# The end of a state-space layer's y (skip term D·xc and gate silu(z)) on ACT and POOL instead of PE and DVE

## The reference, cut to what matters

```
xs, z = split(u @ W_in.T)                  # 192 + 192 channels
xc = silu(causal_conv3(xs) + conv_b)
dt, B, C = split(xc @ W_x.T)               # 6 + 16 + 16
delta = softplus(dt @ W_dt.T + b_dt)
h_t = exp(delta*A) * h_(t-1) + delta*B*xc  # 192 channels x 16 states
y = sum_n h*C  +  xc * D
y = y * silu(z)
out = x + y @ W_out.T
```

## Time and profile before

| | us |
|---|---|
| median of 3 runs (7182.05 to 7199.08) | 7185.96 |
| the profiled execution | 7219.16 |
| its span, first to last instruction | 7217.5 |
| PE busy | 6447.3 |
| DVE busy | 5943.6 |
| ACT busy | 4794.1 |
| POOL busy | 4577.4 |

### The profile page before, as it was taken

The page is one execution under the profiler, slowest core; times in us unless marked ns, Lnnn a source line. Parts: engine busy times, 40 slices in busy tenths (PEclk is TensorE's granted clock), DMA queues, the critical chain, the costliest instruction groups (busy, mean ns, idle before and its releaser), DMA issues. The chain is left out here.

```text
span 7217.5 us, 97516 instructions
## 1 busy us (share of the span) xinstructions
PE 6447.3 (89%) x32099; PEld 3299.1 (46%) x32099; DVE 5943.6 (82%) x4956; ACT 4794.1 (66%) x7986; POOL 4577.4 (63%) x4516
## 2 busy tenths in 40 slices
PE   7898998999898998999999899998999989898765
PEld 5545444444444444444444444444444444444211
DVE  0188888888888888888888888888888888889898
ACT  4576767667676776766667666676766767667554
POOL 0166666666666766667666666666766666677676
PEclk8998989999898998999999898998989999899776
DMA  3465655655655555565655555666555655555552
GB/s 89 112 151 134 146 141 129 148 136 146 148 136 141 140 143 137 145 147 131 150 130 147 143 134 140 138 150 144 136 146 132 150 137 145 144 129 142 121 122 68
DMA packets 805815, 983.15 MB, mean 136 GB/s; under 512 B 391258, under 2 KB 417542, under 8 KB 805318
## 3 DMA queue, kind: packets, MB, share of 16 engines
q1 hardware_dynamic: 805318, 976.92, 56.4%
HBM read 717.71 MB, written 259.00 MB: 135 GB/s over the span
## 5 line engine op out<-in xcount | busy, mean ns | idle before, releaser
L1069 POOL TENSOR_TENSOR hc<-hs,cs 128x512 f32<-128x512 f32 x3072 | 3843.5, 1269 | 2272.8 <-DVE hs L1028 1880.1
L1028 DVE TENSOR_TENSOR_SCAN hs<-av,state,b 128x512 f32<-128x512 f32 x2688 | 3282.4, 1264 | 83.5 <-DVE b L1022 2.7
L1022 DVE TENSOR_TENSOR b<-rep_u,pb 128x1536 f32<-128x1536 f32 x1024 | 1802.8, 1761 | 785.3 <-PE pb L746 721.2
L883 ACT ACTIVATE av<-rep_d,nega 128x512 f32<-128x512 f32 x3072 | 2129.2, 713 | 139.4 <-DVE hs L1028 134.9
L757 PE MATMUL py<-hc,rsel 128*32 128x512 f32 x6144 | 1227.4, 678 | 27.3 <-POOL hc L1069 27.2
L676 PEld LDWEIGHTS cb<-w2c,g 128*98 128x98 f32 x9600 | 937.6, 178 | 330.2 <-issue 267.9
L671 PE MATMUL cb<-xu,w1a 96*128 96x392 f32 x2400 | 1039.9, 529 | 50.1 <-ACT dlt L873 31.0
L676 PE MATMUL cb<-w2c,g 128*98 128x96 f32 x9600 | 990.2, 264 | 83.2 <-issue 55.4
L833 ACT ACTIVATE g<-cb,b1a 128x392 f32<-128x392 f32 x1200 | 695.7, 580 | 205.3 <-PE cb L671 189.5
L746 PE MATMUL pb<-bc,selb 96*128 96x512 bf16 x1024 | 416.4, 407 | 370.0 <-DVE b L1022 368.6
L710 PE MATMUL cb<-xn,wtap 96*96 96x512 f32 x1536 | 701.0, 606 | 0.3 <-DVE spare L966 0.3
(11 more groups left out here) (102 smaller groups left out, 6525.5 us busy)
## 6 DMA issues: line engine op xcount, KB each, us to landing
rep_d<-delta_scratch SPq DMA_DIRECT2D x512, 384.0 KB, 6.2
rep_u<-deltax_scratch SPq DMA_DIRECT2D x512, 384.0 KB, 6.1
cs<-c_scratch SPq DMA_DIRECT2D x512, 256.0 KB, 6.1
delta_scratch<-dlt SPq DMA_DIRECT2D x128, 384.0 KB, 3.1
deltax_scratch<-dlt SPq DMA_DIRECT2D x128, 384.0 KB, 8.1
t_scratch<-t1s SPq DMA_DIRECT2D x128, 300.0 KB
t1r<-t_scratch SPq DMA_DIRECT2D x160, 240.0 KB, 5.0
rr<-v_scratch SPq DMA_DIRECT2D x256, 150.0 KB
```

Of the source, the lines that this page charges most:

```text
L883: act.activation(av[:, n % NAV, :], rep_d[:, k % 2, j, :], ACT.Exp, scale=nega[:, q, j:j + 1])\
L1022: dve.tensor_tensor(b3[:, :, :], rep_u[:, k % 2, 3 * hf:3 * hf + 3, :], pb[:, None, :].broadcast_to([128, 3, T]), ALU.mult).then_inc(dve_b ...
L1028: dve.tensor_tensor_scan(hs[:, n % NHS, :], av[:, n % NAV, :], b3[:, n % 3, :], start, ALU.mult, ALU.add)\
L1069: pool.tensor_tensor(hc[:, n % NHC, :], hs[:, n % NHS, :], cs[:, k % 2, g % NQ, :], ALU.mult)\
```

## The change

`ddiag` and its matmul go; `gate` goes from DVE. In their place:

- ACT scales xc by D in place (Copy with a scale per partition, SBUF to SBUF, both halves) behind its unit 16, one chunk ahead.
- ACT copies `py` (half 0 behind its unit 21, half 1 behind unit 9 of the next chunk) to a new SBUF tile `yv`. PE waits for that copy (`act_y`) before it starts the next half in `py`, where it waited for the gate.
- POOL adds `yv` to the scaled xc and multiplies by `zs`, two instructions in place, behind its unit 17 (half 0) and unit 5 of the next chunk (half 1). OUT and Z's evacuation wait for that (`pool_g`).
- OUT moves in the plan from position 6 to 11, so that ACT evacuates it behind unit 17, and SP stores it and loads `x1o` at its unit 19 instead of 13.

```diff
-    "act": dict(xn=8, mid=23, batch=BATCH + 6),
-    "dve": dict(y0=15, y1=3),
-    "pool": dict(u=23, bc=(16, 21)),
-    "sp": dict(..., x1=21, out=13),
+    "act": dict(xn=8, y=(21, 9), d=16, mid=23, batch=BATCH + 6),
+    "dve": dict(),
+    "pool": dict(u=23, bc=(16, 21), y=(17, 5)),
+    "sp": dict(..., x1=21, out=19),
...
-        rows.append((k * NU + 6, ("PAD", -1) if kind == "first" and k == 0 else ("OUT", k)))
+        rows.append((k * NU + 11, ("PAD", -1) if kind == "first" and k == 0 else ("OUT", k)))
...
                 if q == 0:
-                    pe.wait_ge(dve_y, count(dve_y, G * 2 + hf))
-                    pe.matmul(py[0:C, :], ddiag[:, hf, :], xcs[:, k % 4, hf, :], start=True, stop=False,
-                              skip_group_check=True)
+                    pe.wait_ge(act_y, count(act_y, G * 2 + hf))
                 for j in range(3):
                     mm = pe.matmul(py[32 * j:32 * j + 32, :], rsel[:, :], hc[:, (3 * g + j) % NHC, :],
-                                   start=False, stop=(q == NQ - 1), skip_group_check=True)
+                                   start=(q == 0), stop=(q == NQ - 1), skip_group_check=True)
...
+            def c_part(st, k, n):
+                if n == AT["act"]["d"] and 0 <= st.s * NC8 + k + 1 < NS * NC8:
+
+                    for hf in range(2):
+                        xc = xcs[:, (k + 1) % 4, hf, :]
+                        act.wait_ge(pool_u, count(pool_u, st.s * NC8 + k + 2))
+                        act.activation(xc, xc, ACT.Copy, scale=dskip[:, hf:hf + 1]).then_inc(act_d, 1)
+
+                G = st.s * NC8 + k - (AT["act"]["y"].index(n) if n in AT["act"]["y"] else 0)
+                if n in AT["act"]["y"] and not (G < 0) and not (n == AT["act"]["y"][0] and k == NC8):
+                    hf = AT["act"]["y"].index(n)
+                    act.wait_ge(pool_y, count(pool_y, G * 2 + hf))
+                    act.wait_ge(pe_red, count(pe_red, G * NG + (hf + 1) * NQ))
+                    act.activation(yv[:, :], py[0:C, :], ACT.Copy).then_inc(act_y, 1)
...
-                if n == AT["dve"]["y0"]:
-                    gate(G, k, 0)
-
-            def gate(G, k, hf):
-
-                dve.wait_ge(pe_red, count(pe_red, G * NG + (hf + 1) * NQ))
-                dve.tensor_tensor(xcs[:, k % 4, hf, :], zs[:, k % 2, hf, :], py[0:C, :], ALU.mult).then_inc(dve_y, 1)
...
+                xc = xcs[:, G % 4, hf, :]
+                pool.wait_ge(act_d, count(act_d, G * 2 + 2))
+                pool.wait_ge(act_y, count(act_y, G * 2 + hf + 1))
+                pool.tensor_tensor(xc, xc, yv[:, :], ALU.add).then_inc(pool_y, 1)
+                pool.wait_ge(pool_y, count(pool_y, G * 2 + hf + 1))
+
+                pool.tensor_tensor(xc, xc, zs[:, G % 2, hf, :], ALU.mult).then_inc(pool_g, 1)
```

More of the change, by code:

```diff
@@ L36 @@
     "pe": dict(pb=1, red=5),
-    "act": dict(xn=8, mid=23, batch=BATCH + 6),
-    "dve": dict(y0=15, y1=3),
-    "pool": dict(u=23, bc=(16, 21)),
-    "sp": dict(rd=(1, 2, 3, 5), ru=(6, 8, 10, 12), cs=(15, 16, 17, 18), dl=20, du=4, x1=21, out=13),
+    "act": dict(xn=8, y=(21, 9), d=16, mid=23, batch=BATCH + 6),
+    "dve": dict(),
+    "pool": dict(u=23, bc=(16, 21), y=(17, 5)),
+    "sp": dict(rd=(1, 2, 3, 5), ru=(6, 8, 10, 12), cs=(15, 16, 17, 18), dl=20, du=4, x1=21, out=19),
 }
@@ L114, in plan_of @@
             rows += mamba_rows(k, True)
-        rows.append((k * NU + 6, ("PAD", -1) if kind == "first" and k == 0 else ("OUT", k)))
+        rows.append((k * NU + 11, ("PAD", -1) if kind == "first" and k == 0 else ("OUT", k)))
     if kind == "last":
-        rows.append((NC8 * NU + 6, ("OUT", NC8)))
+        rows.append((NC8 * NU + 11, ("OUT", NC8)))
     return padded(rows)
@@ L185, in build @@
         dskip = sb("dskip", [C, 2])
-        ddiag = sb("ddiag", [C, 2, C])
         selb = sb("selb", [C, NQ, 128], BF16)
@@ L241, in build @@
         os_ = sb("os_", [128, 4, C])
+        yv = sb("yv", [C, T])
         cb = ps("cb", [128, RING, 512])
@@ L290, in build @@
         pe_red = sem("pe_red")
-        dve_y = sem("dve_y")
+        act_y = sem("act_y")
+        act_d = sem("act_d")
+        pool_y = sem("pool_y")
+        pool_g = sem("pool_g")
         out_st = sem("out_st")
@@ L325, in build @@
         SETUP_STEPS = 3
-        N_SETUP = 14
+        N_SETUP = 12
         BEFORE = [alone([("SLD", 0)] + s_steps() + [("SG1", 0), ("SG2", 0)]),
@@ L730, in out @@
                 p = (k - 1) % 4
-                pe.wait_ge(dve_y, count(dve_y, G * 2))
+                pe.wait_ge(pool_g, count(pool_g, G * 2))
                 pe.wait_ge(x1o_ld, count(x1o_ld, G * 16))
@@ L859, in batched @@
                     t = key[2]
-                    act.wait_ge(dve_y, count(dve_y, (G2 - LEAD) * 2))
+                    act.wait_ge(pool_g, count(pool_g, (G2 - LEAD) * 2))
                     act.wait_ge(pe_conv, st.done(i))
@@ L912, in when @@
                 return row[0] + LAG["act"]
-            run(when, unit, step, a_part, lambda st, k, n: None)
+            def c_part(st, k, n):
[10 more added lines that the diff above has]
+                    act.activation(yv[:, :], py[0:C, :], ACT.Copy).then_inc(act_y, 1)
+            run(when, unit, step, a_part, c_part)
         @block.vector
@@ L940, in _ @@
                                         cwb.rearrange("c (p t k) -> c k t p", t=2, k=3)[:, tap], ALU.mult))
-            for t in range(2):
-                setup(dve.tensor_scalar(ddiag[:, t, :], ident[0:C, 0:C], dskip[:, t:t + 1], None, ALU.mult))
             dve.wait_ge(setup_a, count(setup_a, 2))
@@ L1029, in unit @@
                     .then_inc(dve_h, 1)
-                if n == AT["dve"]["y0"]:
-                    gate(G, k, 0)
-            def gate(G, k, hf):
-                dve.wait_ge(pe_red, count(pe_red, G * NG + (hf + 1) * NQ))
-                dve.tensor_tensor(xcs[:, k % 4, hf, :], zs[:, k % 2, hf, :], py[0:C, :], ALU.mult).then_inc(dve_y, 1)
[L1038 to L1043, removed]
+            run(lambda row: row[0] + LAG["dve"], unit, step, lambda st, k, n: None, lambda st, k, n: None)
         @block.gpsimd
@@ L1102, in a_part, with c_part @@
                     pool.tensor_tensor(dlt[:, :, :], dlt[:, :, :], xcs[:, k2 % 4], ALU.mult).then_inc(pool_u, 1)
-            run(lambda row: row[0] + LAG["pool"], unit, step, a_part, lambda st, k, n: None)
+            def c_part(st, k, n):
+                if n not in AT["pool"]["y"]:
+                    return
+                hf = AT["pool"]["y"].index(n)
+                G = st.s * NC8 + k - hf
+                if G < 0 or (hf == 0 and k == NC8):
+                    return
+                xc = xcs[:, G % 4, hf, :]
[4 more added lines that the diff above has]
+                pool.tensor_tensor(xc, xc, zs[:, G % 2, hf, :], ALU.mult).then_inc(pool_g, 1)
+            run(lambda row: row[0] + LAG["pool"], unit, step, a_part, c_part)
 def resampling():
```

## The result

The changed kernel takes 7226.5 us (median of 18 runs, 7172.3 to 7282.8) and the kernel before, in runs beside them, 7189.5. The ratio is 1.0048, with a 95% interval of 1.0033 to 1.0064: 0.5% slower, where I had forecast 1.6% faster. One of the 18 runs, that of 7282.8 us, lies over 1.5% above the fastest and counts as slow; the ratio is taken over the other 17. The profiled execution has a span of 7244.9 us at a mean granted clock of 0.89; before it was 0.91.

The account below looks back on a forecast made before the run. PE and DVE were taken to hold each other through the one `pb` bank. Per chunk -2.0 + 0.8 + 0.3 = -0.9 us, times 128, plus 2.4 once: 7186 - 113 = 7073 us, range 6955 to 7215.

Parts of the forecast that it names:

- The scaling, 0.8 us a chunk: ACT's two scalings by D delay the evacuation PE needs at OUT: bounds 0 and 1.6 us a chunk, middle taken.
- the worked chunk: Chunk 0, worked step by step between spreads of B: waits 5.55 us against 6.49, chunk 2.1 us shorter with the gates.
- The base, -2.0 us a chunk: Gain on PE and DVE from dropping diagonal matmul and gate and moving OUT: between 1.14 and 2.0 us, 2.0 taken.
- SP's store and load move with OUT and cost nothing: On SP, OUT's store and the load of `x1o` come six units later: priced at nothing.
- POOL and the copies, 0.3 us a chunk: ACT's copies of `py` and POOL's four instructions a chunk: bounds 0 and 1.3 us, taken near the lower end.
- the fifth rival: POOL feeds PE late at `reduce` behind unit 5 or 20, a 2.5 us pair in most chunks: up to 7390; chance 0.08.
- The third: Behind the batch, OUT and ACT's late evacuation cost 1.6 + 0.3 us a chunk nearly everywhere: about 7173; chance 0.20.
- The fourth: PE waits ahead of group 3's spread, so the batch (X, Z) runs partly at half clock: about 7285; chance 0.12.
- the prediction's own paragraph on the clock: After PE waits, its records run at half clock (1.2 GHz); so a batch could start at half clock.

Follow-up runs that it names:

- the kernel with the scalings out of the way: Changed kernel with ACT's two scalings by D behind unit 14 instead of 16: 7059.4 us, ratio 0.9807 to the kernel before.

## Why the prediction was wrong

Two terms of the sum were mis-sized, and both in the hopeful direction. Per chunk I had -2.0 + 0.8 + 0.3.

- **The scaling, 0.8 us a chunk, was 1.36** (174 us over 128 against the place behind unit 14). This is the step that failed: the rows gave a bound of 1.6 us in the worked chunk, the wait came out at 1.45 and 1.71, and I took the middle for want of the other chunks. I also priced only the wait. The waits themselves are some 0.5 us a chunk, which is below the middle; the half clock behind them adds up to 0.9 (both estimates, from the two ways of splitting above). The longer W_2 record of chunk 3 is that part.
- **The base, -2.0 us a chunk, with POOL's 0.3 was to give -218 us; the kernel with the scalings out of the way gives -139.** The worked chunk 0 and chunk 1 of the earlier trace rows stood for all eight. By chunk, that kernel gains 1.7 to 3.6 us in chunks 1, 2, 4, 6 and 7, 0.5 in chunk 3, 0.1 in chunk 0, and loses 2.9 in chunk 5. The diagonal matmul alone brings 92 us and not 256: in chunks 0, 5 and 6 nothing is left of it, and a later stretch of each runs longer at a lower clock. In the worked chunk 0, where I forecast 2.1 us, the last stretch is 1.8 us longer with the scalings at 14 (10.1 against 8.3 on average), its granted clock 0.67 against 0.90; what lowers the clock there is open. And about 3 us of each chunk 5, some 45 us in all, go to the wait for `rr`, which I had not seen: I wrote that SP's store and load move with OUT and cost nothing, and did not ask what OUT and the diagonal matmul had covered on PE.
- Either error alone would have stayed in the range: 7073 + 72 = 7145 and 7073 + 79 = 7152. Together they are 7224. That this meets the measured 7226.5 confirms nothing, since both are measured against the same kernel, the one with the scalings at 14, and must add up to the difference. What the scalings cost behind unit 14 themselves, if anything, counts in the base.
- **POOL and the copies, 0.3 us a chunk:** right in kind. The addition alone measures 0.2 to 0.3 us; the multiplication and the copies were not measured by themselves. The POOL instructions take 1.27 us each where the earlier trace rows gave 1.18 to 1.25, and POOL stands at 5194 us (5200 forecast). PE's matmuls wait 125 us for `hc` instead of 49, one wait 3.6 us at the longest, where the kernel before had the same longest, so the fifth rival came in small and not as 2 us in most chunks.
- **The rivals.** The third named the place, and put a price of 1.9 us on it in nearly every chunk; the wait came in half of the chunks, and its time, 7173, was short by the clock and by chunk 5. The fourth named the mechanism, half clock behind a wait that the change makes, but at the batch. Of the batches only chunk 5's shows it newly, for part of X, and behind the wait for `rr` (granted clock 0.86 on average, 1.00 before); those of chunks 4 and 7 ran partly at half before too. Had I joined the two, the prediction's own paragraph on the clock would have warned of it: a wait of 1.5 us on PE can cost more by what follows than by its length.
- The Trainium skill ("TensorE: Matmul & The Clock Gate", section "HAM oscillation") has bursts with waits in between fall to half rate again and again. The trace agrees in part: the clock fell after the wait in chunk 3 in nine samples of fourteen and not in five, and with OUT elsewhere the same wait cost no clock in that stretch.

Whether another, unseen term hides in what is left, the runs don't exclude: of the three parts two were measured, on the kernel before (OUT -32 us, diagonal matmul -92), the gate's going was not tried by itself, and they need not add up.

## What to carry to other kernels

Before putting work on a half idle engine, find the one instruction of it that the leading engine waits for next, and put the work behind that, or ahead where the engine still idles; two units' difference was 2.4% here. Work out every distinct chunk of a period, not one of each kind, because a bound from one chunk says nothing of the share of chunks that meet it. When a step is moved away, ask which load or evacuation it had been covering, on the engine that ran it.

## What was not expected of the hardware

- The same 1.71 us wait, followed by the same instructions, left PE at full clock in some samples and brought 1.2 GHz in others, with 8.79 us against 5.63 for 53 matmuls. One profile of one sample would have shown either.
- More than half of what the misplaced scalings cost (by estimate 100 to 115 of 174 us) was lost clock.
- PE work taken out of a chunk did not always shorten it: in chunk 0 2.1 us saved without the diagonal matmul came with a last stretch 1.6 us longer, at a granted clock of 0.70 instead of 0.90.
- A load of 150 KB took 8.5 us on average from issue until PE went on in chunk 5, where the timeline also shows `rep_d` loads and the store of delta*x being issued within 4 us of it; 1.3 us of that went when the store was issued behind the load.
